# The spike count from two staircase activations instead of five signs, and which engine squares what

## What is computed

```python
def ffn(x, W_fc, W_proj):                       # W_fc 512x128, W_proj 128x512
    h = square(relu(einsum('bsd,fd->bsf', x, W_fc)))
    y = einsum('bsf,df->bsd', h, W_proj)
    def step(mem, _):                           # NUM_STEPS = 5
        reset = spike(mem - 1.0)
        mem_new = 0.9 * mem + y - reset
        return mem_new, spike(mem_new - 1.0)
    _, spks = scan(step, zeros_like(y), None, length=5)
    return sum(spks, axis=0) / 5

x = x + 0.5 * ffn(layernorm(x), W_fc, W_proj)
x = x + attention(layernorm(x), ...)            # keys, values, exp weights, two cumulative sums
x = x + 0.5 * ffn(layernorm(x), W_fc, W_proj)
```

## Time and profile before

| | |
|---|---|
| median of 3 runs | 150.46 us (150.0 to 150.66) |
| profiled execution, first to last instruction | 148.4 us |
| what the median has beyond that span | 2.06 us |
| TensorE clock granted | 1.00 of full speed throughout |
| instructions on PE / VectorE / ScalarE / GpSimd | 945 / 437 / 255 / 142 |

### The profile page before, as it was taken

How to read it: one execution, slowest core, us unless ns; L and a number is a source line. 1 busy time by engine, 2 the same in 40 slices (tenths; PEclk the granted TensorE clock), 3 DMA queues, 4 the chain that set the end, 5 groups by cost and what they waited for, 6 DMA issues and landing times.

```text
span 148.4 us, 3010 instructions
## 1 busy us (share of the span) xinstructions
PE 142.6 (96%) x945; PEld 126.7 (85%) x945; DVE 126.4 (85%) x437; ACT 128.6 (87%) x255; POOL 96.8 (65%) x142
## 2 busy tenths in 40 slices
PE   7999999999999999999999999999899999999990
PEld 7799898889889899997988989888789898979790
DVE  3885478689699999999989999999999999464674
ACT  3376989899999998979999999799798997978861
POOL 1448135978799927993999899979953954450200
PEclk9999999999999999999999999999999999999999
DMA  4974000000000000000000000020020011120222
GB/s 140 262 216 142 4 2 0 0 0 7 0 0 0 4 4 0 0 0 0 4 0 2 0 0 4 2 69 2 0 73 4 23 47 35 40 70 0 71 71 71
DMA packets 10510, 5.09 MB, mean 34 GB/s; under 512 B 1152, under 2 KB 10496, under 8 KB 10496
## 3 DMA queue, kind: packets, MB, share of 16 engines
q1 hardware_dynamic: 9808, 4.53, 10.5%
q10 hardware_dynamic: 688, 0.39, 0.9%
HBM read 2.82 MB, written 2.10 MB: 33 GB/s over the span
## 4 chain that ended last, share of the span: by engine, by line
PE 68%; DVE 13%; ACT 8%; issue 4%; DMA 3%; POOL 2%; ACTq 1%; DVEq 0%
PE work L1000 28%; PE hidden L921 8%; PE hidden L925 8%; PE hidden L922 7%; PE work L934 3%; DMA proj_raw<-in_L_ffn_W_proj_dram 3%; ACT signs L517 2%; PE att_work L1031 2%; PE att_value L1055 2%; ACT square L494 2%; PE att_work L921 2%; DVE stats_att L599 2%; PE att_work L922 2%; PE att_work L925 2%; DVE weight_sum L763 2%
## 5 line engine op out<-in xcount | busy, mean ns | idle before, releaser
L1000 PE MATMUL work<-proj_t,square 128*128 128x128 f32 x480 | 61.7, 276 | 0.1
L1000 PEld LDWEIGHTS work<-proj_t,square 128*128 128x128 f32 x480 | 59.1, 192 | 2.9 <-POOL square L422 0.5
L517 ACT ACTIVATE signs<-work 128x512 uint8<-128x512 f32 x73 | 41.3, 619 | 5.3 <-PE work L1000 5.3
L489 ACT ACTIVATE relu<-hidden 128x512 f32<-128x512 f32 x64 | 37.9, 626 | 0.0
L494 ACT ACTIVATE square<-relu 128x512 f32<-128x512 f32 x53 | 35.5, 669 | 0.3
L921 PE MATMUL hidden<-in_hi,fc_lo 128*128 128x512 f32 (+1 forms) x66 | 27.6, 418 | 0.1
L925 PE MATMUL hidden<-in_lo,fc_hi 128*128 128x512 f32 (+1 forms) x66 | 25.6, 389 | 0.0
L922 PE MATMUL hidden<-in_hi,fc_hi 128*128 128x512 f32 (+1 forms) x66 | 25.4, 385 | 0.0
L401 POOL TENSOR_TENSOR rstd<-var_eps,minus_half 128x4 f32<-128x4 f32 x15 | 15.3, 1021 | 14.6 <-DVE neg_mean L612 14.6
L407 POOL TENSOR_SCALAR normed_att<-x_att,neg_mean_att,rstd_att 128x128 f32<-128x128 f32 x32 | 18.3, 585 | 0.8
L672 DVE TENSOR_TENSOR in_lo<-work,in_hi 128x512 fp32r<-128x512 f32 x15 | 10.2, 678 | 9.1 <-ACT in_hi L485 9.1
(11 more groups left out here) (117 smaller groups left out, 252.3 us busy)
## 6 DMA issues: line engine op xcount, KB each, us to landing
x_first<-_attn_hidden_states_dram SPq DMA_DIRECT2D x7, 256.0 KB, 4.3
out_dram<-x_out SPq DMA_DIRECT2D x7, 256.0 KB, 2.2
out_dram<-x_out SPq DMA_DIRECT2D x4, 64.0 KB, 1.5
x_first<-_attn_hidden_states_dram ACTq DMA_DIRECT2D x1, 128.0 KB, 2.7
x_first<-_attn_hidden_states_dram SPq DMA_DIRECT2D x1, 128.0 KB, 2.4
fc_raw<-in_L_ffn_W_fc_dram SPq DMA_DIRECT2D x1, 128.0 KB, 2.7
fc_raw<-in_L_ffn_W_fc_dram ACTq DMA_DIRECT2D x1, 128.0 KB, 3.1
proj_raw<-in_L_ffn_W_proj_dram SPq DMA_DIRECT2D x1, 128.0 KB, 3.7
```

Source lines behind the costliest of these rows:

```text
L489: nc.scalar.activation(relu[j.lane][:, c, :], bank_of_hidden(j, c)[:], ACT.Relu).then_inc(relu_made[j.lane], 1)
L517: nc.scalar.activation(signs[j.lane][:, k, :], work[j.lane][:], func, bias=bias, scale=scale).then_inc(signs_made[j.lane], 1)
L1000: last = nc.tensor.matmul(work[j.lane][:, tokens], square[j.lane][:, c, tokens], proj_t[:, c, :], start=(c == 0 and t == 0), stop=(c == NC ...
```

## The change

The count comes from two activations and two VectorE operations. The first activation (`Prelu`: one slope above zero, another below) is a bent line that, rounded to a 16-bit integer on the write, steps at the first three levels; the second (`Copy` with scale and bias) is a straight line that steps at levels four and five. The larger of the two, clamped to 4 and increased by 1, is the count. All squares are ScalarE's in jobs 0 to 13; job 14 keeps chunk 1 on VectorE and gives chunk 0 from GpSimd to ScalarE; job 15 keeps its split (GpSimd 0, VectorE 1 and 2, ScalarE 3). The buffers `signs` and `sign_sum` (8 bits) are replaced by `stairs`, `highest` and `count` (16 bits). The core of the diff:

```diff
-DVE_SQUARES = [(0,), ()]
+DVE_SQUARES = [(), ()]
 NEXT_TO_LAST_DVE_SQUARES = (1,)
 LAST_SQUARES = {"pool": (0,), "dve": (1, 2), "act": (3,)}
-POOL_SQUARES = [(0,), ()]
-SIGN_ADDS = [4, 4]
-POOL_SIGN_ADDS = [0, 0]
+POOL_SQUARES = [(), ()]
+STAIRS_A_JOB = 2
...
+def bent_form(lowest, low, high):
+
+
+    scale, bias = line_form(low, high, 0.5)
+    under, over = (float(stepped(scale, v, bias)) for v in (lowest, after(lowest)))
+    slope = float(np.float32(-1 / (under + over)))
+    assert under < over < 0 and np.float32(slope * under) < -0.5 < np.float32(slope * over)
+    return scale, bias, slope
 
...
     SPIKE_LEVELS = spike_levels()
-    LEVELS = [sign_form(level) for level in SPIKE_LEVELS]
-    NL = len(LEVELS)
-    STAIRS = [(ACT.Relu, pair_form(*SPIKE_LEVELS[0:2])), (ACT.Sign, LEVELS[4]),
-              (ACT.Relu, pair_form(*SPIKE_LEVELS[2:4]))]
+    BENT_SCALE, BENT_BIAS, BENT_SLOPE = bent_form(*SPIKE_LEVELS[0:3])
+    LINE_SCALE, LINE_BIAS = line_form(*SPIKE_LEVELS[3:5], 2.5)
...
-        signs = [sb(f"signs{l}", [P, NL, S], U8) for l in LANES]
-        sign_sum = [sb(f"sign_sum{l}", [P, S], U8) for l in LANES]
+        stairs = [sb(f"stairs{l}", [P, STAIRS_A_JOB, S], I16) for l in LANES]
+        highest = [sb(f"highest{l}", [P, S], I16) for l in LANES]
+        count = [sb(f"count{l}", [P, S], U16) for l in LANES]
...
+            def bent_stair(out, y):
+                return nc.scalar.activation(out, y, ACT.Prelu, bias=BENT_BIAS, scale=BENT_SCALE, alpha=BENT_SLOPE)
+
+            def line_stair(out, y):
+                return nc.scalar.activation(out, y, ACT.Copy, bias=LINE_BIAS, scale=LINE_SCALE)
+
+            def last_stairs():
                 for t in range(NT):
                     tokens = slice(t * P, (t + 1) * P)
                     act.wait_ge(y_tile_made, t + 1)
...
+                    bent_stair(stairs[last_lane][:, 0, tokens], y_tiles[t][:, 0:P]).then_inc(stairs_tile_made, 1)
+                    line_stair(stairs[last_lane][:, 1, tokens], y_tiles[t][:, 0:P]).then_inc(stairs_tile_made, 1)
+
+            def ff_stairs(j):
+                if j.turn:
+                    act.wait_ge(highest_made[j.lane], j.turn)
                 if j.is_last:
...
+                    last_stairs()
                     return
...
+                act.wait_ge(y_made[j.lane], j.turn + 1)
+                bent_stair(stairs[j.lane][:, 0, :], work[j.lane][:]).then_inc(stairs_made[j.lane], 1)
+                line_stair(stairs[j.lane][:, 1, :], work[j.lane][:]).then_inc(stairs_made[j.lane], 1)
...
                 for j in feed_forward(i - 1):
...
+                    ff_stairs(j)
...
                     ff_square(j, 0)
-                for j in feed_forward(i - 1):
-                    ff_sign(j, 2)
...
+            def last_highest(j, t):
                 tokens = slice(t * P, (t + 1) * P)
...
+                dve.wait_ge(stairs_tile_made, STAIRS_A_JOB * (t + 1))
+                nc.vector.tensor_tensor(highest[j.lane][:, tokens], stairs[j.lane][:, 0, tokens],
+                                        stairs[j.lane][:, 1, tokens], ALU.max).then_inc(highest_tile_made, 1)
+
+            def last_count(j, t):
                 tokens = slice(t * P, (t + 1) * P)
...
+                dve.wait_ge(highest_tile_made, t + 1)
+                nc.vector.tensor_scalar(count[j.lane][:, tokens], highest[j.lane][:, tokens], SPIKE_STEPS - 1.0, 1.0,
+                                        ALU.min, ALU.add).then_inc(count_tile_made, 1)
 
             def last_add(j, t):
                 tokens = slice(t * P, (t + 1) * P)
...
+                dve.wait_ge(count_tile_made, t + 1)
+                nc.vector.scalar_tensor_tensor(x_of["out"][j.batch][:, t, :], count[j.lane][:, tokens],
                                                RESIDUAL_STEP, x_of["second"][j.batch][:, t, :], ALU.mult,
                                                ALU.add).then_inc(x_tile_made, 1)
 
...
+            def ff_highest(j):
                 if j.is_last:
...
                     return
...
+                dve.wait_ge(stairs_made[j.lane], STAIRS_A_JOB * (j.turn + 1))
+                if j.turn:
+                    dve.wait_ge(count_made[j.lane], j.turn)
+                nc.vector.tensor_tensor(highest[j.lane][:], stairs[j.lane][:, 0, :], stairs[j.lane][:, 1, :],
+                                        ALU.max).then_inc(highest_made[j.lane], 1)
+
+            def ff_count(j):
+                if j.is_last:
+                    for t in range(NT):
+                        last_highest(j, t)
+                        last_count(j, t)
+                        last_add(j, t)
                     return
...
+                dve.wait_ge(highest_made[j.lane], j.turn + 1)
+                for last in feed_forward(j.index - 2):
+                    dve.wait_ge(x_made[NEXT[last.layer]], last.batch + 1)
+                nc.vector.tensor_scalar(count[j.lane][:], highest[j.lane][:], SPIKE_STEPS - 1.0, 1.0, ALU.min,
+                                        ALU.add).then_inc(count_made[j.lane], 1)
 
             def ff_add(j):
                 if j.is_last:
                     return
 
-                wait_sums(dve, j, j.sign_adds)
+                dve.wait_ge(count_made[j.lane], j.turn + 1)
                 nc.vector.scalar_tensor_tensor(
-                    flat(x_of[NEXT[j.layer]][j.batch]), sign_sum[j.lane][:], RESIDUAL_STEP,
+                    flat(x_of[NEXT[j.layer]][j.batch]), count[j.lane][:], RESIDUAL_STEP,
                     flat(x_of[j.layer][j.batch]), ALU.mult, ALU.add).then_inc(x_made[NEXT[j.layer]], 1)
...
-                for j in feed_forward(i - 2):
-                    ff_sum_sign(j, 3)
...
-                for j in feed_forward(i - 2):
-                    ff_sum_sign(j, 4)
...
                 for j in feed_forward(i - 1):
-                    ff_sum_sign(j, 1)
+                    ff_highest(j)
...
                 for j in feed_forward(i - 1):
-                    ff_sum_sign(j, 2)
+                    ff_count(j)
...
                 if j.turn:
-                    pe.wait_ge(signs_made[j.lane], j.before(lambda other: other.sign_parts))
+                    pe.wait_ge(stairs_made[j.lane], STAIRS_A_JOB * j.turn)
...
```

More of the change, by code:

```diff
@@ L27 @@
 F32R = mybir.dt.float32r
-U8, U16, I32 = mybir.dt.uint8, mybir.dt.uint16, mybir.dt.int32
-I32 = mybir.dt.int32
+I16, U16, I32 = mybir.dt.int16, mybir.dt.uint16, mybir.dt.int32
 ALU = mybir.AluOpType
@@ L109, in spike_levels @@
     return levels
-def sign_form(level):
-    ulp = 2.0 ** (int(np.floor(np.log2(level))) - 23)
-    middle2 = 2 * int(float(level) / ulp) + 1
-    for k in range(1, 4096):
-        scale = 2**23 + k
-        product = scale * middle2
-        bias = float(np.float32(product * ulp * 2.0**-24))
-        off = abs(int(bias / ulp * 2.0**24) - product)
-        if off < 2**21:
-            return scale * 2.0**-23, -bias
-    raise ValueError("no scale separates the two")
 def inverse_form():
@@ L148, in inverse_form, with after, stepped, line_form @@
     return log_scale, log_bias, root, centre, c0 - centre**2
-def pair_form(low, high):
-    def after(value):
-        return np.uint32(int(value.view(np.uint32)) + 1).view(np.float32)
-    def stepped(scale, value, bias):
-        return np.float32(float(scale) * float(value) + float(bias))
+def after(value):
+    return np.uint32(int(np.float32(value).view(np.uint32)) + 1).view(np.float32)
+def stepped(scale, value, bias):
+    return np.float32(float(scale) * float(value) + float(bias))
+def line_form(low, high, first):
     near = int(np.float32(1 / (float(high) - float(low))).view(np.uint32))
@@ L328, in bank_of_hidden @@
             return hidden[(NC * j.index + c) % HIDDEN_BANKS]
-        def wait_sums(engine, j, upto):
-            engine.wait_ge(sign_sum_made[j.lane], j.before(lambda other: other.sign_adds) + upto)
-        def wait_sum_read(engine, j):
-            for last in feed_forward(j.index - 2):
-                engine.wait_ge(x_made[NEXT[last.layer]], last.batch + 1)
         def wait_dve_square(engine, j, c):
@@ L576, in _ @@
                     ff_relu(j, 2)
-                for j in feed_forward(i - 1):
-                    ff_sign(j, 3)
-                    ff_sign(j, 4)
                 for j in feed_forward(i):
```

102 lines of the change are left out of this document (8 added, 94 removed).

## The result

The changed kernel takes **148.0 us** (median of 6 runs, 147.38 to 149.8) where the kernel before takes 150.45 on the same chip (6 runs): a ratio of 0.9845, interval 0.9813 to 0.9877. A later set of runs gave 148.54 against 150.79, 0.9831 (0.9784 to 0.9878). The gain is 2.45 us where 3.6 were forecast, inside the range of 146.1 to 148.7. The profiled execution took 147.76 us with a span of 146.0, a clock of 0.999 and one table load. Executions of one kernel lie up to 2.4 us apart at a clock of 0.995 or more, which widens the intervals; part of that lies ahead of TensorE's first 512-column product, which starts between 9.17 and 10.45 us in the thirteen traces.

The account below looks back on a forecast made before the run. TensorE bounds the kernel on average, VectorE sets the pace in full attention steps. Terms of 0.53, 0.28, 1.3, 0.51 and 0.65, less 0.1, plus 0.4 scattered, gave 3.6 us and so 146.9 us; range 146.1 to 148.7.

Parts of the forecast that it names:

- first attention turn: TensorE's wait at the first attention turn, 0.53 us, goes entirely because the attention statistics on VectorE start earlier.
- second: TensorE's two waits at the second attention turn, 0.11 and 0.17 us, together 0.28, go as ScalarE's squares come earlier.
- weight_key: Attention turns waiting for VectorE's `weight_key`: three waits shrink from 1.3 to 0.1 us in total.
- jobs 13 and 14: TensorE's waits at the contractions of jobs 13 and 14, 0.51 us, go as late squares come earlier.
- last job and tail: The last job's contraction waits (0.43 us) and the time after the last product: together 0.25 to 0.85 gained, 0.65 taken.
- scattered: Six or seven short TensorE waits elsewhere from 9 us on, 0.05 to 0.1 us each, counted as 0.4 gained.
- in a row they cost 0.20 each: VectorE's four removed additions per job, 0.306 us long, were priced at 0.20 each, 0.8 us per step.
- 2.65 us after y, and TensorE asks after 2.8: ScalarE's first moved square is done 2.65 us after y is complete; TensorE asks for it about 2.8 us after y.
- The squares at no cost: Seven squares moved to ScalarE cost nothing; with stairs 0.2 us longer, each of seven steps would wait some 0.2.
- One table load as before: Against the slower rival: new ScalarE functions need two 1.28 us table loads per attention step, 7.2 us in all, 154.1; chance 0.03.
- no 8-bit rate: Against the rival that VectorE's maximum and clamp get no packed rate and take 0.69 us each: 149.0 us; chance 0.09.
- `weight_key` stays ahead of GpSimd's normalisation: Against the rival that attention turns come to wait for GpSimd's normalisation, costing 1.0 us: 147.9 us; chance 0.11.

Follow-up runs that it names:

- fourth_place_add: The changed kernel with one unused 256-column 16-bit addition per job on VectorE, where the removed fourth addition had stood: 148.54 us, the same median as the changed kernel.
- count_in_the_gap: The changed kernel with the count of jobs 0 to 13 moved to the removed third addition's place, behind an attention step's statistics: 147.13 us, ratio 0.9769.
- job14_square_on_vector: The changed kernel with VectorE squaring hidden block 0 of job 14 instead of block 1: 147.39 us, ratio 0.9808.
- scalar_load_back: The changed kernel with three unused signs per job on ScalarE, in the places of the removed third, fourth and fifth: 152.8 us, ratio 1.0143.
- squares_only: The kernel before, still with five signs per job, with the squares of jobs 0 to 13 and job 14's chunk 0 on ScalarE: 152.08 us, ratio 1.0101.

## Why the prediction was right or wrong

*The whole.* Forecast 146.9, measured 148.0. The mechanism held: fewer activations let squares and turns come in time, and VectorE falls behind less; a third of the forecast gain did not come, and the range was wide enough to hold that. Waits on TensorE are read as in the prediction, from the distance of two starts. Taken start by start over the 902 instructions from the first 512-column product on, the kernel after has 2.63 us less. It came to that product 0.18 us later (9.43 for 9.25), an accident of that execution, so the span is 2.44 shorter. By terms:

| term | forecast | trace |
|---|---|---|
| first attention turn | 0.53 | 0.53 |
| second | 0.28 | 0.28 |
| `weight_key` | 1.2 | 0.64 |
| jobs 13 and 14 | 0.51 | 0.30 |
| last job and tail | 0.65 | 0.30 |
| scattered | 0.4 | 0.58 |

*`weight_key`, the largest miss.* The step that failed is "in a row they cost 0.20 each": I read 0.20 from one addition, which stood between independent operations, and applied it to four. Two of the four, the first and the third, stood behind statistics whose result the next operation waits for, and cost nothing. So the additions cost 0.40 a step, not 0.80. The new pair costs less than my 0.5 too: the maximum took the first one's place (0.59 from statistics to reduction instead of 0.47, so 0.12) and the count costs 0.20. The residual addition got 0.08 shorter. 10.45 - 0.40 + 0.32 - 0.08 = 10.29; measured 10.27, forecast 10.15. `fourth_place_add` and `count_in_the_gap` show it from both sides. The 0.08 is luck, and not the 16-bit counts: the same addition in the kernel after and in `fourth_place_add`:

```profile
95.75 0.70 DVE L693 SCALAR_TENSOR_TENSOR x_out<-count,x_second 128x512 f32<-128x512 uint16 x1
```

```profile
96.11 0.78 DVE L699 SCALAR_TENSOR_TENSOR x_out<-count,x_second 128x512 f32<-128x512 uint16 x1
```

It takes 0.68 to 0.69 us where nothing of GpSimd's runs beside it, with 8-bit counts too, and up to 0.9 beside a GpSimd normalisation. In `fourth_place_add` that makes 0.07 of the 0.27 us by which the step is longer.

*Single durations* were right: maximum 0.416 us for 0.42, count 0.29 for 0.3, stairs 0.594 for 0.62. The estimates from the Trainium skill's page "VectorE: DVE Perf Modes" (§ The perf-mode tier table), 0.42 and 0.29, agree with them.

*Jobs 13 and 14.* Job 13's 0.21 went. For job 14 the step "2.65 us after y, and TensorE asks after 2.8" was off. ScalarE's first stair starts at 128.72 and its square 0, the fifth in the row, ends at 131.31; TensorE's twelve products would let it go on at 131.24. The 2.8 were counted from the start of the last contraction, while y is complete only at its end, 0.27 later. `job14_square_on_vector` removed the wait.

*The last job and the tail.* The 0.43 went, as forecast. The 0.22 for the tail did not come: I took 0.45 + 3 x 0.31 for a tile, free VectorE assumed, and named the rate of a tile as what could spoil it. It did: tiles 0 and 1 come 0.39 apart and the others 0.67, and at 0.69 a tile VectorE is still late for the last. And 0.12 us were lost at the first contraction, which waits for GpSimd's square: 138.55 - 138.00 = 0.55 instead of 0.43. It began 0.68 us ahead of the last product before (139.45, 140.13) and 0.61 ahead now (137.39, 138.00), and took 1.11 us instead of 1.06; that makes the 0.12.

*The range.* Its lower end stands for "all of 4.3 us of waits gone", but the terms don't add up to 4.3: the waits listed are 3.45, and 3.87 with the upper 0.85 for last job and tail.

*The squares at no cost.* Right but for job 14, and the cover was thinner than the text had it. I allowed 0.2 us more per stair, and priced its loss at some 0.2 in seven steps, 1.4 us. `scalar_load_back` lost 4.8 us against the kernel after, with 1.3 us more busy time per job on ScalarE (132.2 to 113.8 in all), 3.5 of it by the list of waits in eleven waits for squares.

*The rivals.* One table load as before, no 8-bit rate, and `weight_key` stays ahead of GpSimd's normalisation as what attention turns wait for: fallen. The rule of the Trainium skill's page "ScalarE: Activation LUTs" (Rules for kernel authors), multiplications on VectorE, is neither wrong nor right by the duration: the square takes 641 ns on ScalarE here and took 749 on VectorE, a mean in which one took 1.15 us beside a GpSimd square and seven of nine 0.68 to 0.69. The page gives a rate for bf16 operations with one source as its reason, which this fp32 product of two inputs is not. What decides is which engine has time at that moment: with five signs the move costs 1.5 us (`squares_only`), with two stairs it gains 0.5 in the trace, and for chunk 0 of job 14 VectorE is the better place again.

## What to carry to other kernels

Price an instruction to be removed by what lies between its neighbours, not by its duration: if the next one waits for a result from before it, it is free, and the gap it leaves is a place to put other work. Where each operation of a short chain reads the one before it, lay another chain's operation between them. A wait list of before doesn't price an engine's relief once other work is moved onto it; put the load back and look.

## What the hardware showed that I had not expected

A VectorE operation with two 16-bit inputs that started behind a two-input GpSimd product of 512 columns lasted until 0.14 to 0.30 us after that one's end. Where it began 0.12 to 0.13 us behind it, in four cases, 0.28 became 1.31 and 1.29 us for 256 columns, and 0.42 became 1.26 for 512 (twice). The kernel before has it too, in four of its additions, which began late in such a product and so lost less. The longest took 0.50 us and ended 0.14 after the product:

```profile
39.09 1.30 POOL L450 TENSOR_TENSOR guess_share<-weight_key,guess 128x512 f32<-128x512 f32 x1
...
40.03 0.50 DVE L749 TENSOR_TENSOR sign_sum<-sign_sum,signs 128x256 uint16<-128x256 uint16 x1
```

fp32 squares of VectorE that began 0.44 us behind a GpSimd square ended 0.55 us after it and took up to 1.22 us instead of 0.69. The Trainium skill's page "GPSIMD Engine Reference" (its table of SBUF interfaces) says that GpSimd contends with VectorE instructions that are in a 2-port mode or have two SBUF inputs. With its two-input half the trace agrees. The count, with one input, stood beside a GpSimd product in ten of the traces and kept its 0.26 to 0.29 us, but it had begun 0.06 to 0.08 us earlier each time, so no run here shows what a one-input operation does behind one. The price in these traces is the whole rest of GpSimd's operation, so it depends on when the two begin. And two VectorE instructions of which the second reads the first's result stand 0.11 us apart behind the layer statistics of full batches where nothing else fills it; in one place of the kernel after it is 0.48, for a reason that the trace does not name.
